# Cross attention whose weights are turned by a DMA transpose and divided after the product

## The chip, the cores and the metric

The kernel runs on one core of a Trainium2 chip. Its engines are TensorE (PE: matrix products, with their weight loads shown apart as PEld), VectorE (DVE), ScalarE (ACT), GpSimd (POOL) and SyncE (SP), which here issues transfers. The metric is the device time of one execution in microseconds, as the median of several runs.

## The reference

Sixteen sequences of 128 tokens with 128 features go through two decoder layers. Layer 0 has self attention (16 heads of 8), cross attention (8 heads of 64) and a quantised feed forward step; layer 1 has self attention, cross attention (16 heads of 64) and a mixture of 8 experts. What matters here is the cross attention of each layer:

```
q = split_heads(x @ Wq);  k = split_heads(context @ Wk);  v = split_heads(context @ Wv)
sim = einsum('bhid,bhjd->bhij', q, k) * scale
attn = softmax(sim, axis=-1)
out = einsum('bhij,bhjd->bhid', attn, v)
return out (heads side by side) @ Wo + bo
```

The second layer's is the same without scale and bias. All inputs and the output are float32.

## The kernel before

A sequence is one tile of 128 tokens by 128 features. Every sequence passes the stages self0, cross0, ffn, self1, cross1 and moe, and several sequences are under way at once. A step of the kernel is named stage.step.group: `cross1.pv.0` is the product of weights and values for the first group of eight heads in cross1. cross0 has one such group, cross1 two, so there are 48 groups in all (16 sequences by 3); the text calls one of them a unit.

The order of the steps on each engine is written out by hand in the table `ORDER` (two characters a step). At build time the class `Plan` replays the table with the costs of `all_steps()` to give each result its bank of PSUM (eight banks); the engines then run their lists in order, and semaphores make them wait.

The steps of a unit before the change are these. `s1` (PE, line 1257): scores of eight heads, 128 queries by 128 keys each. `mx` (DVE, line 980): the negative maximum of a row. `ex` (ACT, line 805): eight exponentials of 128x128. `rc` (DVE, lines 987 and 989): sum and reciprocal. `nz` (POOL, line 728): the exponentials times the reciprocal. `t` (PE, line 1270): each head's weights are turned, eight 128x128 turns into PSUM. `wT` (ACT, line 813): a copy of the turned weights to SBUF. `pv` (PE, line 1297): values times turned weights, in float32, two heads in the two halves of the array's columns ("64 columns"). `oTe` (ACT): a copy to SBUF. `y` and `z` (PE, line 1335): the output projection.

PE can divide its array into parts. The scores of the cross attention use 64 rows, those of the self attention 32, the old product 64 columns, all else the whole array; `array_parts()` says which step uses which, and `switch()` what the plan charges for a change.

The values come from `v` (PE, lines 1316 to 1318: three products of 512 columns) and `ve` (ACT copy). `AHEAD` says for how many sequences keys and values are held. SP issues the loads at the start, and then waits for each finished sequence to store it (line 669).

Of the kernel before, what the change touches and what calls it, by code (L numbers as in the profile page):

```python
# [6 lines left out]
F32 = mybir.dt.float32  # L7
# [7 lines left out]
P = 128  # L15
NSEQ = 16
SH, SD = 16, 8
XD = 64
# [13 lines left out]
AHEAD = dict(cross0=8, cross1=6)  # L32
EARLY = 4
WARM = 9

class Step:

    def __init__(self, engine, cost, after, again, bank, until, parts, once, half, first, last):
# [42 lines left out]
def all_steps():  # L82
    steps = {}

    def add(name, engine, cost, after=(), again=(), bank=None, until=None, parts=1, once=False, half=0, first=None,
            last=None):
        steps[name] = Step(engine, cost, after, again, bank, until, parts, once, half, first, last)
# [44 lines left out]
    def keys_values(L, chunks, k_w, v_w):  # L132
# [4 lines left out]
        for c in range(chunks):  # L137
            fill(f"{L}.v.{c}", 695, [*context, f"{v_w}.lo"], f"{L}.ve.{c}", [ago(f"{L}.pv.{c}", AHEAD[L])])
            add(f"{L}.ve.{c}", "ACT", 484, [f"{L}.v.{c}"])

    def cross_attention(L, source, chunks, following, biased, k_w, v_w, loads):
# [5 lines left out]
        for c in range(chunks):  # L147
            add(f"{L}.s1.{c}", "PE", 893, [f"{L}.qe.{c}", second(f"{L}.ke.{c}")], [f"{L}.t.{c}"], "S", f"{L}.ex.{c}")
            add(f"{L}.mx.{c}", "DVE", 1130, [f"{L}.s1.{c}"])
# [16 lines left out]
    add("consts", "POOL", 2700, once=True)  # L166
    for name, load, engine, hi, lo in (("ctx0", "c0", "DVE", 530, 610), ("b_k", "b_k", "DVE", 530, 610),
# [7 lines left out]
    add("self0.bi", "POOL", 412, ["self0.res", "in.more"], [ago("cross0.res", 2)])  # L175
# [21 lines left out]
    add("moe.o", "DVE", 198, ["moe.b", "moe.sm"])  # L197
    return steps
# [12 lines left out]
        "aHaJa4a4aOa4aLa6a4aHa6aQaJa6aUa6bYbqbWbWbYbWaXaObYaLb2b2aZaUbYb0aHaQaJb0b0b0a1a6aXaObaa4aLaHbcaJaZaQ"  # L211
        "bea1aUa6b2a4b0a4aXaObabWaLbjbcaUaHblaZaQaJbebnbWa1aXbYbWaOaZbwa4a1aLa4bab2bcbybjaHaUbeblbCaQbGbEbabn"
        "bYaJaXbcbJaZaLb2bja1bebwblaHa6bya4a6bQaObCa6bEbna6baaUbSbjbcbUbGaQbJblb6bebwb8bybnccb0aXbCcabQaLaJbE"
        "claZaHbGbSbUa1chbjbJcjblb6bacqb8bwcabycccla4bncsbQaOb2bWaJbcbSaQa6bCcubUbEaUchbWbwcvbybeb6cqcaaXbJcs"
        "aZb8aLbGaHcza1clcccja4cCcDcubjcvbQb2aObCaJa4bSblcHbaaUa6czbcbUbEbncCaQchbeb6bGcDbJaXcacLb8cqaLbwcHcl"
        "cjcsccbQcuaZaHbycva1bWbYbSbjbUaOblbaaJbYbCbcaUbEcLczbnaQbWcCcqcDbGchb6bebJcscjbwcaaXb8cHbyclccaZa4a1"
        "bQcua6bjaLaHcvaObCaJblbEb0aQbGbnbaczbSaUcqcCbUbcchbJcsbeaXcLbwb6cDcaaZb8a1bycHclcjccbQbWb2cucLcvbSbj"
        "bUaLaOblbCb0babEbnaQczaHbcbGaUcCcDaJb6cqb8bebJcsaXchcaaLbwcccjaZbyclaHa1cua6cvbja4bQaOblbScHa4aJbnba"
        "aQczbcaUbCcCcqbUbEcDcLchbebJcscjaXb6bGbWb8aZcacHaLa1ccclbwcubyaHcvbjbYbQaOblbSbCb2bUbEbaaQbccLbnchb6"
        "aUczb8bGcCcabebJcjbYcDcqccclcsaXcucHbwcvaZbybQaJbjaLb0b0a1blaObCa6aHbEbna6bSaQcLbYczaJbUbGbaaUcCchcD"  # L220
        "bccqb6bwbebJaXcab8cjcsccaZaLbyclcHcua1aHcvbjbYb0aOblbQb2bnbaaUbcczaQchcCaJcqbSbeaXbUcLcDcscjaOaZb6b0"
        "bCcab8bGa1aLaQbEccaUbwclbjbybYcuaXcvblbJaZb2babncHczbccqa1cCbecsbCcLcDbYbabQbcbGcHchbSbEcLbUbjcjbJbe"
# [1306 lines left out]
```

## Time and profile before

| | |
|---|---|
| median of 3 runs | 499.45 us (499.38 to 499.49) |
| span of the profiled execution | 497.5 us |
| PE busy | 488.7 us (98%) |
| ACT busy | 437.1 us (88%) |
| DVE busy | 400.1 us (80%) |
| POOL busy | 371.4 us (75%) |
| granted TensorE clock | 1.000 |

The span runs from the first to the last instruction of one profiled execution; the time of a run includes what lies around it. The profile's share of an engine is its busy time by the span. PE counts as busy from the start of a product to its modelled end, and products overlap, so how long a group of them takes is read from the start of the group to the start of what follows it. The chain of waits goes back from the last instruction, at each step to what released it.

### The profile page before, as it was taken

To read this page: it belongs to the slowest core of one execution; us is meant where nothing else is said; L and a number is where in the kernel's file an instruction comes from. 1 tells how busy PE (TensorE), PEld (TensorE's weight loads), DVE (VectorE), ACT (ScalarE), POOL (GpSimd) and SP (SyncE) were. 2 spreads that over 40 slices of the span, in tenths; PEclk is the share of its full clock that TensorE was granted. 3 is DMA by queue.
4 is the path that set the end of the run, shared out by engine and by line. 5 is a ranking of instruction groups with operands and counts; after the bars stand their busy time and mean duration, and the time that the engine had idled before them with its cause. 6 is when DMAs were issued, how large, how long until landed. Compare 5 with 4: busy or idle time off the path is not lost.

```text
span 497.5 us, 15713 instructions
## 1 busy us (share of the span) xinstructions
PE 488.7 (98%) x5510; PEld 416.8 (84%) x5510; DVE 400.1 (80%) x906; ACT 437.1 (88%) x1180; POOL 371.4 (75%) x455
## 2 busy tenths in 40 slices
PE   8999999999999999999999999999999999999996
PEld 4778887888888888889889888888888898988885
DVE  5767778897888888989898898878898687876665
ACT  5988889999998898998898898989789899989782
POOL 2876677897868887788768886976869688568754
PEclk9999999999999999999999999999999999999999
DMA  6800000000000000000000000000000000000000
GB/s 196 336 2 1 3 1 3 1 2 3 1 3 1 7 2 9 1 3 7 7 3 1 8 3 5 4 7 1 4 7 1 8 7 3 7 3 2 7 7 16
DMA packets 6460, 8.64 MB, mean 17 GB/s; under 512 B 1392, under 2 KB 4848, under 8 KB 6384
## 3 DMA queue, kind: packets, MB, share of 16 engines
q1 hardware_dynamic: 5952, 6.86, 4.1%
q8 instruction: 45, 0.74, 0.6%
q10 hardware_dynamic: 432, 0.79, 0.5%
q14 instruction: 31, 0.25, 0.2%
HBM read 6.50 MB, written 1.05 MB: 15 GB/s over the span
## 4 chain that ended last, share of the span: by engine, by line
PE 90%; ACT 4%; DVE 2%; SPq 1%; issue 1%; DMA 1%; POOL 1%; DVEq 0%; POOLq 0%; ACTq 0%
PE psum L1270 14%; PE psum L1257 10%; PE psum L1297 10%; PE psum L1213 8%; PE psum L1335 8%; PE psum L1244 6%; PE psum L1283 3%; PE psum L1461 3%; PE psum L1347 3%; PE psum L1308 2%; PE psum L1285 2%; PE psum L1316 2%; PE psum L1310 2%; PE psum L1318 2%; PE psum L1317 2%; PE psum L1309 2%
## 5 line engine op out<-in xcount | busy, mean ns | idle before, releaser
L723 POOL TENSOR_TENSOR w_self<-w_self 128x1024 f16<-128x1024 f32 x64 | 121.2, 1901 | 27.3 <-ACT w_self L794 13.8
L805 ACT ACTIVATE w_cross<-psum,row_max_cross 128x128 f32<-128x128 f32 x384 | 104.4, 408 | 5.5 <-DVE row_max_cross L980 4.6
L728 POOL TENSOR_TENSOR w_cross<-w_cross,e_rec_cross 128x1024 f32<-128x1024 f32 x48 | 91.0, 1898 | 20.6 <-DVE e_rec_cross L989 20.6
L980 DVE TENSOR_REDUCE row_max_cross<-psum 128x8 f32<-128x1024 f32 x48 | 58.0, 1215 | 13.6 <-PE psum L1257 12.8
L987 DVE TENSOR_REDUCE e_sum_cross<-w_cross 128x8 f32<-128x1024 f32 x48 | 58.2, 1213 | 4.5 <-ACT w_cross L805 4.2
L1257 PE MATMUL psum<-kT_cross,qT_cross 64*128 64x128 f32 x768 | 54.4, 283 | 0.0
L1297 PEld LDWEIGHTS psum<-w_cross,v_cross 128*64 128x64 f32 x768 | 41.1, 136 | 14.3 <-issue 11.0
L813 ACT ACTIVATE w_cross<-psum 128x1024 f32<-128x1024 f32 x48 | 49.9, 1043 | 3.3 <-PE psum L1270 3.2
L1257 PEld LDWEIGHTS psum<-kT_cross,qT_cross 64*128 64x128 f32 x768 | 46.3, 187 | 6.8 <-issue 4.9
L1297 PE MATMUL psum<-w_cross,v_cross 128*64 128x128 f32 x768 | 51.4, 278 | 0.3 <-ACT w_cross L813 0.3
L1270 PE MATMUL psum<-ident,w_cross 128*128 128x128 f32 x384 | 49.8, 274 | 0.1
L1270 PEld LDWEIGHTS psum<-ident,w_cross 128*128 128x128 f32 x384 | 43.1, 142 | 1.4 <-ACT by_head_self L770 0.3
L998 DVE TENSOR_TENSOR w_self<-psum,row_max_self 128x1024 f32<-128x1024 f32 x32 | 39.2, 1225 | 2.4
L996 DVE TENSOR_REDUCE row_max_self<-psum 128x8 f32<-128x1024 f32 x32 | 38.9, 1215 | 1.3 <-PE psum L1244 1.0
L1007 DVE SCALAR_TENSOR_TENSOR w_self<-psum,s_bound 128x1024 f32<-128x1024 f32 x32 | 37.8, 1216 | 2.5 <-PE psum L1244 2.4
L788 ACT ACTIVATE w_self<-w_self,shift 128x1024 f32<-128x1024 f32 x32 | 36.9, 1160 | 2.4 <-DVE w_self L1007 2.4
L770 ACT ACTIVATE by_head_self<-psum,head_mask 128x128 f32<-128x128 f32 x128 | 37.3, 405 | 0.0
L1244 PE MATMUL psum<-by_head_self,plain_self 32*128 32x512 f32 x256 | 36.5, 639 | 0.2 <-issue 0.2
L794 ACT ACTIVATE w_self<-psum 128x1024 f32<-128x1024 f32 x32 | 33.1, 1035 | 4.0 <-PE psum L1270 3.5
L770 ACT ACTIVATE attnT_cross<-psum 128x512 f32<-128x512 f32 x48 | 29.7, 622 | 6.8 <-PE psum L1297 6.3
L1335 PE MATMUL psum<-e_o,attnT_cross 128*128 128x128 f32 x256 | 34.3, 277 | 0.0
L1270 PE MATMUL psum<-ident,w_self 128*128 128x128 f32 x256 | 33.5, 274 | 0.5 <-DVE w_self L998 0.4
(213 smaller groups left out, 1377.0 us busy)
## 6 DMA issues: line engine op xcount, KB each, us to landing
out_dram<-x_all SPq DMA_DIRECT2D x16, 64.0 KB, 1.6
x_all<-in_x SPq DMA_DIRECT2D x1, 768.0 KB, 7.2
cT_all<-in_ctx SPq DMA_DIRECT2D x1, 768.0 KB, 9.4
e_k<-in_e_k SPq DMA_DIRECT2D x1, 512.0 KB, 4.9
e_v<-in_e_v SPq DMA_DIRECT2D x1, 512.0 KB, 5.8
e_q<-in_e_q SPq DMA_DIRECT2D x1, 512.0 KB, 8.6
e_o<-in_e_o SPq DMA_DIRECT2D x1, 512.0 KB, 9.5
m_w<-in_m_w SPq DMA_DIRECT2D x1, 512.0 KB, 8.5
```

Of the source, the lines that this page charges most:

```text
L723: pool.tensor_tensor(L.w_low[u], L.w[u][:], halves(L.w[u][:]), ALU.subtract)\
L728: pool.tensor_tensor(L.diff[u][:].rearrange("p (h k) -> p h k", h=UNIT), L.e[u][:].rearrange("p (h k) -> p h k", h=UNIT), L.e_rec[:, u, :] ...
L770: act.activation(dst, src, ACT.Copy, **scale).then_inc(emptied(i, name)[0], 1)
L805: last = act.activation(L.e[u][:, P * p:P * (p + 1)], S_[:, P * p:P * (p + 1)], ACT.Exp, bias=L.row_max[:, u, p:p + 1])
L813: act.activation(L.w[u][:], group(i, turn)[:], ACT.Copy).then_inc(taken(i, turn)[0], 1)
L980: dve.tensor_reduce(L.row_max[:, u, :], group(i, turn)[:].rearrange("p (h k) -> p h k", h=UNIT), AX_X, ALU.max, negate=True).then_inc(L.ma ...
L987: dve.tensor_reduce(L.e_sum[:, u, :], L.e[u][:].rearrange("p (h k) -> p h k", h=UNIT), AX_X, ALU.add)
L1244: last = pe.matmul(group(i, name, u)[:, 512 * half:512 * (half + 1)], L.plain[rows, :], L.by_head[rows, :, :].rearrange("p j n -> p (j n)" ...
L1257: last = pe.matmul(S_[:, at:at + P], L.qT[rows, h // 2, :], kT[rows, h // 2, i % 2, :], start=True, stop=True)
L1270: last = pe.transpose(S_[:, P * k:P * (k + 1)], L.diff[u][:, P * k:P * (k + 1)], ident[:])
L1297: last = pe.matmul(bank(i, name)[rows, P * pair:P * (pair + 1)], v[:, h, :], L.w[c][:, P * place(h):P * (place(h) + 1)], start=True, stop= ...
L1335: last = pe.matmul(bank(i, y)[:, 0:P], L.attnT[:, k, :], L.o_w[:, k, :], start=k == 0 and not with_x, stop=k == 4 * L.chunks - 1)
```

## The change

`rc`, `nz`, `t` and `wT` go. After `ex` a unit now has these steps. `hi` (ACT): the exponentials, not divided, rounded to 16 bits. `lo` (POOL): what the rounding left, also in 16 bits. `dm` (SP): one DMA transpose turns both planes, 128 by 2048 elements of 16 bits (512 KB), SBUF to SBUF, into 16 blocks of 128x128. `pv` (PE): three products a head, 24 a unit, with a turned 16-bit plane as the loaded tile and the values as the streamed columns: high plane by high values (64 columns and a column of ones, which gives the sum of the weights), high plane by low values (64), low plane by high values (65). Queries now lie on partitions. `nr` (DVE): reciprocal of the sums, and a multiplication by it. `T` (PE): four 128x128 turns of the float32 result, then `oTe` as before.

The values are held as a 16-bit high part (`ve`, ACT) and a 16-bit low part (the new `vl`, DVE), with the ones set once at the start by POOL. Values and keys are held for 6 and 4 sequences instead of 8 and 6. The result before its turn lies in the memory of the turned planes. `x_bias` shares memory with a loaded weight. The transposes and the stores are now in SP's written-out list. All tables of `ORDER` are new; one line of each stands below.

```diff
-AHEAD = dict(cross0=8, cross1=6)
+AHEAD = dict(cross0=6, cross1=4)
+TURN, TURN_TAIL = 2100, 1300
...
+            add(f"{L}.vl.{c}", "DVE", 605, [f"{L}.ve.{c}"])
...
-            add(f"{L}.ex.{c}", "ACT", 2060, [f"{L}.mx.{c}"], [f"{L}.pv.{c}"], half=1030)
-            add(f"{L}.rc.{c}", "DVE", 1401, [f"{L}.ex.{c}"])
-            add(f"{L}.nz.{c}", "POOL", 1856, [f"{L}.rc.{c}"])
-            add(f"{L}.t.{c}", "PE", 874, [f"{L}.nz.{c}"], (), "S", f"{L}.wT.{c}")
-            add(f"{L}.wT.{c}", "ACT", 914, [f"{L}.t.{c}"])
-            fill(f"{L}.pv.{c}", 873, [f"{L}.wT.{c}", f"{L}.ve.{c}"], f"{L}.oTe.{c}", [f"{L}.{'yz'[c]}"])
-            add(f"{L}.oTe.{c}", "ACT", 486, [f"{L}.pv.{c}"])
+            add(f"{L}.ex.{c}", "ACT", 2060, [f"{L}.mx.{c}"], [f"{L}.lo.{c}"], half=1030)
+            add(f"{L}.hi.{c}", "ACT", 940, [f"{L}.ex.{c}"], [f"{L}.dm.{c}"])
+            add(f"{L}.lo.{c}", "POOL", 1856, [f"{L}.hi.{c}"])
+            add(f"{L}.dm.{c}", "SP", TURN, [f"{L}.lo.{c}"], [f"{L}.T.{c}"], tail=TURN_TAIL)
+            add(f"{L}.pv.{c}", "PE", 740, [f"{L}.dm.{c}", f"{L}.vl.{c}", "ones"], (), "S", f"{L}.nr.{c}")
+            add(f"{L}.nr.{c}", "DVE", 930, [f"{L}.pv.{c}"])
+            fill(f"{L}.T.{c}", 437, [f"{L}.nr.{c}"], f"{L}.oTe.{c}")
+            add(f"{L}.oTe.{c}", "ACT", 486, [f"{L}.T.{c}"], [f"{L}.{'yz'[c]}"])
...
 ORDER = dict(
     PE=(
-        "aHaJa4a4aOa4aLa6a4aHa6aQaJa6aUa6bYbqbWbWbYbWaXaObYaLb2b2aZaUbYb0aHaQaJb0b0b0a1a6aXaObaa4aLaHbcaJaZaQ"
+        "aIaKa5aMa5aPaIa5a7a5a7aRa7bZaVbtb1aKa7bZb1aYaPbZa0b6b1aMa2aVb3b6aIaRb1aKb3b3a7bca5aYaPaMa7aIbeaKb3aR"
...
-    return ("64 columns",) * 2 if step == "pv" and L in ("cross0", "cross1") else ("", "")
+    return "", ""
...
+            def turn(L, i, u):
+                sp.wait_ge(L.e_low[u], i + 1)
+                if i:
+                    sp.wait_ge(x_full, full(i - 1, f"{L.name}.T.{u}"))
+                sp.dma_start_transpose(L.eT[u][:], L.e_parts[u][:]).then_inc(L.e_turned[u], 16)
...
-            def divide_by_sum(L, i, u):
-                pool.wait_ge(L.rec_ready[u], i + 1)
...
+            def low_weights(L, i, u):
+                pool.wait_ge(L.e_high[u], i + 1)
+                pool.tensor_tensor(L.e_parts[u][:, UN:2 * UN], L.e[u][:], L.e_parts[u][:, 0:UN], ALU.subtract)\
+                    .then_inc(L.e_low[u], 1)
...
-            def weights_by_key(L, i, u):
-                turn = f"{L.name}.t.{u}"
-                act.wait_ge(s_full, score(i, turn))
-                act.activation(L.w[u][:], group(i, turn)[:], ACT.Copy).then_inc(taken(i, turn)[0], 1)
+            def high_weights(L, i, u):
+                act.wait_ge(*taken(i, f"{L.name}.s1.{u}"))
+                if i:
+                    act.wait_ge(L.e_turned[u], 16 * i)
+                act.activation(L.e_parts[u][:, 0:UN], L.e[u][:], ACT.Copy).then_inc(L.e_high[u], 1)
...
+            def divide_by_sums(L, i, u):
+                name = f"{L.name}.pv.{u}"
+                sums = by_head(group(i, name))
+                rec = L.e_rec[:, u, :].rearrange("p (z h) -> p z h", z=2)
+                dve.wait_ge(s_full, score(i, name))
+                dve.reciprocal(rec, sums[:, :, :, XD])
+                dve.drain()
+                dve.tensor_tensor(L.attn[u].rearrange("p (z h w) -> p z h w", z=2, w=XD), sums[:, :, :, 0:XD],
+                                  rec.unsqueeze(3).broadcast_to([P, 2, UNIT // 2, XD]), ALU.mult)\
+                    .then_inc(taken(i, name)[0], 1)
...
-                pe.wait_ge(*taken(i, f"{L.name}.t.{c}"))
+                pe.wait_ge(L.e_turned[c], 16 * (i + 1))
                 room(i, name)
...
+                for h in range(UNIT):
+                    e_high, e_low = L.eT[c][:, place(h), :], L.eT[c][:, UNIT + place(h), :]
+                    at = 512 * (h // 4) + (XD + 1) * (h % 4)
+                    pe.matmul(out_[:, at:at + XD + 1], e_high, v_high[:, UNIT * c + h, :], start=True, stop=False)
+                    pe.matmul(out_[:, at:at + XD], e_high, v_low[:, UNIT * c + h, :], start=False, stop=False)
+                    last = pe.matmul(out_[:, at:at + XD + 1], e_low, v_high[:, UNIT * c + h, :], start=False, stop=True)
+                last.then_inc(s_full, 1)
```

The order on PE near the end, in the kernel before: from the projection of sequence 14 in cross1 (line 1335, `y` and `z`) to the last sequence's first product. w0 and w1 are the weights of the two head groups, v3 the values, lines 1316 to 1318 make values.

```order
L1335 MATMUL psum<-e_o,attnT_cross1 128x128 x4
L1316 MATMUL psum<-e_v_hi,cT_all_lo 128x512
L1317 MATMUL psum<-e_v_lo,cT_hi 128x512
L1318 MATMUL psum<-e_v_hi,cT_hi 128x512
L1335 MATMUL psum<-e_o,attnT_cross1 128x128 x4
L1270 MATMUL psum<-ident,w0_cross1 128x128 x8
L1448 MATMUL psum<-m_b,g_weightT 128x128
L1270 MATMUL psum<-ident,w1_cross1 128x128 x8
L1297 MATMUL psum<-w0_cross1,v3_cross1 64x128 x8
```

And in the kernel after, from the end of sequence 14's second product to the start of the last sequence's first. eT0 and eT1 hold the turned planes, and later the result that line 1367 turns; line 1404 is the projection.

```order
L1487 MATMUL psum<-m_g,moe_xnT 128x8
L1367 MATMUL psum<-ident,eT1_cross1 128x128 x4
L1519 MATMUL psum<-m_b,g_weightT 128x128
L1367 MATMUL psum<-ident,eT0_cross1 128x128 x4
L1404 MATMUL psum<-e_o,attnT_cross1 128x128 x8
L1358 MATMUL psum<-v_high3_cross1,eT0_cross1 128x65
```

The turns of the weights and the making of values have left this place; four turns of a result a group, which wait for DVE, stand ahead of the projection, and the first of 24 products of the last sequence directly behind it.

The order on ACT at the same place, before: the exponentials of the last sequence's two head groups (line 805), and the copies of its turned weights (line 813).

```order
L805 ACTIVATE w0_cross1<-psum,row_max_cross1 128x128 x8
L770 ACTIVATE attnT_cross1<-psum 128x512
L805 ACTIVATE w1_cross1<-psum,row_max_cross1 128x128 x8
L770 ACTIVATE g_weightT<-psum 128x128
L770 ACTIVATE attnT_cross1<-psum 128x512
L770 ACTIVATE v3_cross1<-psum 128x512 x2
L915 ACTIVATE psum,g_sum<-logits,g_negmax 128x8
L813 ACTIVATE w0_cross1<-psum 128x1024
```

And after; line 860 rounds the exponentials to 16 bits into e_parts.

```order
L851 ACTIVATE w0_cross1<-psum,row_max_cross1 128x128 x8
L860 ACTIVATE e_parts0_cross1<-w0_cross1 128x1024
L851 ACTIVATE w1_cross1<-psum,row_max_cross1 128x128 x8
L860 ACTIVATE e_parts1_cross1<-w1_cross1 128x1024
L816 ACTIVATE attnT_cross1<-psum 128x512 x2
```

The 1024-element step of a head group moved from behind PE's turns to directly behind its exponentials, and the two copies of sequence 14's result (attnT) stand behind both groups now.

## Rows read from the trace of the kernel before

**Rows 1.** The page: busy time of PE, and the chain that ended last, by engine.

```profile
PE 488.7 (98%) x5510; PEld 416.8 (84%) x5510; DVE 400.1 (80%) x906; ACT 437.1 (88%) x1180; POOL 371.4 (75%) x455
...
PE 90%; ACT 4%; DVE 2%; SPq 1%; issue 1%; DMA 1%; POOL 1%; DVEq 0%; POOLq 0%; ACTq 0%
```

**Rows 2.** Stretches: us, busy of PE, PEld, DVE, ACT, POOL, clock, DMA share, GB/s.

```profile
200.00:300.00 100.00, 100.00 (x1204) 87.55 (x1201) 87.50 (x195) 90.80 (x254) 82.43 (x103) 1.00 0.02 4
...
20.00:470.00 450.00, 447.75 (x5193) 385.68 (x5192) 372.27 (x808) 406.75 (x1103) 348.23 (x419) 1.00 0.02 7
470.00:497.50 27.50, 23.64 (x207) 19.21 (x205) 16.30 (x50) 16.59 (x50) 14.09 (x18) 1.00 0.04 10
```

**Rows 3.** Timeline of PE from 251 us: start, duration, engine, line, operation.

```profile
251.46 1.09 PE L1297 MATMUL psum<-w_cross,v_cross 128*64 128x128 f32 x16
252.48 0.19 PE L1283 MATMUL psum<-v_self,w_self 128*128 128x27 bf16 x1
...
253.28 0.17 PE L1285 MATMUL psum<-v_self,w_self 128*128 128x18 bf16 x1
253.31 1.07 PE L1270 MATMUL psum<-ident,w_cross 128*128 128x128 f32 x8
254.22 1.06 PE L1213 MATMUL psum<-xnT_cross,e_q 128*128 128x128 f32 x8
```

**Rows 4.** Timeline of PE from 278 us: two old products in a row.

```profile
278.64 1.97 PE L1297 MATMUL psum<-w_cross,v_cross 128*64 128x128 f32 x32
280.54 0.19 PE L1283 MATMUL psum<-v_self,w_self 128*128 128x27 bf16 x1
```

**Rows 5.** Chain of waits from 475 us: two products of 512 columns.

```profile
475.84 0.23 PE psum L1428
476.07 0.23 PE psum L1429
```

**Rows 6.** Groups by line: busy us, mean ns, idle before; steps that go.

```profile
L728 POOL TENSOR_TENSOR w_cross<-w_cross,e_rec_cross 128x1024 f32<-128x1024 f32 x48 | 91.0, 1898 | 20.6 <-DVE e_rec_cross L989 20.6
L813 ACT ACTIVATE w_cross<-psum 128x1024 f32<-128x1024 f32 x48 | 49.9, 1043 | 3.3 <-PE psum L1270 3.2
L987 DVE TENSOR_REDUCE e_sum_cross<-w_cross 128x8 f32<-128x1024 f32 x48 | 58.2, 1213 | 4.5 <-ACT w_cross L805 4.2
L989 DVE RECIPROCAL e_rec_cross<-e_sum_cross 128x8 f32<-128x8 f32 x48 | 9.7, 203 | 3.5
```

**Rows 7.** Groups by line: rows nearest to the steps that come.

```profile
L723 POOL TENSOR_TENSOR w_self<-w_self 128x1024 f16<-128x1024 f32 x64 | 121.2, 1901 | 27.3 <-ACT w_self L794 13.8
L1084 DVE TENSOR_TENSOR weighted<-psum,g_weight 128x1024 f32<-128x1024 f32 x15 | 18.3, 1222 | 1.2 <-PE psum L1429 0.4
L843 ACT ACTIVATE e_k_hi<-e_k 128x1024 fp32r<-128x1024 f32 x1 | 1.1, 1061 | 0.6 <-DMA e_k<-in_e_k 0.6
L618 DVE TENSOR_TENSOR b_k_lo<-b_k,b_k_hi 128x512 fp32r<-128x512 f32 x1 | 0.7, 693 | 0.3 <-ACT b_k_hi L843 0.3
```

**Rows 8.** The page: GB/s by slice; transfers: KB, us from issue to landing.

```profile
GB/s 196 336 2 1 3 1 3 1 2 3 1 3 1 7 2 9 1 3 7 7 3 1 8 3 5 4 7 1 4 7 1 8 7 3 7 3 2 7 7 16
...
out_dram<-x_all SPq DMA_DIRECT2D x16, 64.0 KB, 1.6
...
e_k<-in_e_k SPq DMA_DIRECT2D x1, 512.0 KB, 4.9
...
e_o<-in_e_o SPq DMA_DIRECT2D x1, 512.0 KB, 9.5
```

**Rows 9.** Groups by line: exponentials and maximum, which stay.

```profile
L805 ACT ACTIVATE w_cross<-psum,row_max_cross 128x128 f32<-128x128 f32 x384 | 104.4, 408 | 5.5 <-DVE row_max_cross L980 4.6
L980 DVE TENSOR_REDUCE row_max_cross<-psum 128x8 f32<-128x1024 f32 x48 | 58.0, 1215 | 13.6 <-PE psum L1257 12.8
```

**Rows 10.** Chain of waits near the end: the last sequence's first scores and turns.

```profile
470.69 1.09 PE psum L1257 x16
...
480.27 0.97 PE psum L1270 x8
```

More of the change, by code:

```diff
@@ L31, with __init__ @@
 BANKS = 8
-AHEAD = dict(cross0=8, cross1=6)
+AHEAD = dict(cross0=6, cross1=4)
 EARLY = 4
+TURN, TURN_TAIL = 2100, 1300
 WARM = 9
 class Step:
-    def __init__(self, engine, cost, after, again, bank, until, parts, once, half, first, last):
+    def __init__(self, engine, cost, after, again, bank, until, parts, once, half, first, last, tail):
+        self.tail = TAIL[engine] if tail is None else tail
         self.first = cost if first is None else first
@@ L85, in add @@
     def add(name, engine, cost, after=(), again=(), bank=None, until=None, parts=1, once=False, half=0, first=None,
-            last=None):
-        steps[name] = Step(engine, cost, after, again, bank, until, parts, once, half, first, last)
+            last=None, tail=None):
+        steps[name] = Step(engine, cost, after, again, bank, until, parts, once, half, first, last, tail)
     def fill(name, cost, after, until, again=(), parts=1, once=False, last=None):
@@ L166, in all_steps @@
     add("consts", "POOL", 2700, once=True)
+    add("ones", "POOL", 1000, ["consts"], once=True)
     for name, load, engine, hi, lo in (("ctx0", "c0", "DVE", 530, 610), ("b_k", "b_k", "DVE", 530, 610),
@@ L174, in all_steps @@
     self_attention("self0", "self0.st", True, "cross0", "in.first", "in.more")
-    add("self0.bi", "POOL", 412, ["self0.res", "in.more"], [ago("cross0.res", 2)])
+    add("self0.bi", "POOL", 412, ["self0.res", "in.more", since("tern.make", 1)], [ago("cross0.res", 2)])
     cross_attention("cross0", "self0.res", 1, "ffn", ["self0.bi"], "b_k", "b_v", "in.more")
@@ L346, in __init__ @@
             idle[engine] = now + cost
-            ended[i, name] = now + cost + TAIL[engine]
+            ended[i, name] = now + cost + s.tail
             self.before[i, name] = []
@@ L396, in __init__ @@
             self.diff = self.w
-            self.diff_ready = [self.sem(f"diff_ready{u}") for u in range(units)]
+            if heads == SH and width == SD:
+                self.diff_ready = [self.sem(f"diff_ready{u}") for u in range(units)]
         else:
@@ L666, in _, with store, do_step @@
                         sp.dma_start(mask[j][0:32 * j, :], mask[0][P - 32 * j:P, :]).then_inc(masks_turned, 16)
-            for i in range(NSEQ):
+            def turn(L, i, u):
[3 more added lines that the diff above has]
+                sp.dma_start_transpose(L.eT[u][:], L.e_parts[u][:]).then_inc(L.e_turned[u], 16)
+            def store(i):
                 sp.wait_ge(*emptied(i, "moe.b"))
                 sp.dma_start(out[i], x_all[:, i, :]).then_inc(stored, 16)
+            def do_step(i, name, L, step, u):
+                if step == "dm":
+                    turn(L, i, u)
+                if step == "out":
+                    store(i)
+            run("SP", do_step)
             sp.wait_ge(stored, 16 * NSEQ)
@@ L754, in do_step @@
                     cut_v(L, i)
-                if step == "lo":
+                if step == "lo" and L in (self0, self1):
                     low(L, i, u)
-                if step == "nz":
-                    divide_by_sum(L, i, u)
+                if step == "lo" and L in (cross0, cross1):
+                    low_weights(L, i, u)
                 if step == "bi":
```

199 lines of the change are left out of this document (112 added, 87 removed).

## The prediction

> **What bounds the kernel now.** I read the page's busy shares first, then the chain of waits: PE is busy 488.7 of 497.5 us, and 90% of the chain that ended last is PE, 4% ACT [rows 1]. Then the stretches: between 200 and 300 us PE has no idle time at all, while ACT is busy 90.8 and DVE 87.5 of 100 us [rows 2]. So PE's own work sets the pace, what comes off PE comes off the time, and ACT is next, about 10% behind. The end differs: from 470 us PE is busy 23.6 of 27.5 us [rows 2].
>
> The profiled span is 497.5 us and the median of the timed runs 499.45, so 1.95 us lie around the span. I keep them.
>
> **The change part by part.** A "unit" is one head group of one sequence; there are 48 (16 sequences, one group in cross0 and two in cross1). What a unit did between the exponentials and the projection is replaced.
>
> *PE, removed.* The eight turns of the weights: start of the turns to start of what follows is 253.31 to 254.22, so 0.91 us [rows 3]; 48 x 0.91 = 43.7 us. The old product: one group alone takes 251.46 to 252.48, 1.02 us [rows 3], two in a row 278.64 to 280.54, 1.90 us [rows 4]. So a product is 0.88 us, and 0.14 us goes to changing the array's division (64 columns before, whole array behind). 48 x 0.88 = 42.2 us. Together 85.9 us.
>
> *PE, added.* 24 products a unit, each with a whole 16-bit 128x128 tile to load and 65 or 64 columns to stream. The trace has no such product. Its nearest is the self attention's: 16-bit tiles of the same size with 27 and 18 columns, 32 of them from 252.48 to 253.31 [rows 3], 26 ns each. A streamed column costs 0.23 us / 512 = 0.45 ns [rows 5], so 65 columns are 29 ns. The lower bound is 26 ns, as if the columns were free; the upper is 26 + 29 = 55 ns, load and columns one after the other. The 512-column products next to each other show their loads hidden, so I take the larger of the two and 1 ns, 30 ns: 24 x 30 = 0.72 us, 48 x 0.72 = 34.6 us (30 to 63). Then four turns a unit of the result, half of the old eight: 0.455 us, 21.8 us. Added 56.4, net 29.5 us less.
>
> *PE, changes of division.* The new product uses the whole array. Counted in the two written-out orders, PE changes its division 190 times before and 156 times after; 34 x 0.14 = 4.8 us less. PE's work becomes 488.7 - 29.5 - 4.8 = 454.4 us.
>
> *ACT.* The copy of the turned weights out of PSUM goes (49.9 us), and a 16-bit copy of the exponentials comes. Nearest row: a 128x1024 copy from SBUF, 1.06 us [rows 6, 7]. 48 x 1.06 = 50.9, so ACT stays at 438 us. The copy of the values changes only its type.
>
> *DVE.* The sum (58.2) and its reciprocal (9.7) go [rows 6]. The low part of the values comes, 128x512, 0.69 us as the same subtraction takes now, or half of 1.22 us from PSUM, 0.61 [rows 7]; and a division of 128x512, likewise 0.69, behind a reciprocal of 0.20. 48 x (0.69 + 0.69 + 0.20) = 75.8 against 67.9: DVE grows from 400 to 408 us, still far from PE.
>
> *POOL.* The multiplication at 1898 ns goes [rows 6]; a subtraction of the same shape comes, 1901 ns [rows 7]. No change; setting the columns of ones is once, at the start, beside the loads.
>
> *The transposes.* 48 SBUF-to-SBUF transfers of 512 KB, issued by SP. Behind one in SP's queue stand only other transposes and the stores of finished sequences; nobody waits for a store but the end. The wait that counts is PE's, before the product. The trace has no transposing transfer. Bounds by the nearest rows: 1.6 us for a 64 KB store, 9.5 us for 512 KB among other loads; a 512 KB load that met less traffic took 4.9 us [rows 8]. With 1.6 us of fixed part and 448 KB at the 336 GB/s of the loading phase [rows 8], 1.3 us, it would be 2.9; between 2.9 and 4.9 I take 3.5 us. Queue time is no issue: 48 x 3.5 = 168 us of the span. In the middle PE has other sequences' work between the scores and the product, so the transfer hides there: what is late next is only the latency.
>
> *Latency, where it shows.* From scores to product it was maximum 1.2, exponentials 2.2 (104.4 us / 48), sum and reciprocal 1.4, multiplication 1.9, then PE's turns and ACT's copy [rows 6, 9]. Now it is 1.2 + 2.2 + 1.06 + 1.9 + 3.5 = 9.9 us. At the end PE runs out of other work. In the order after, between the last sequence's first scores and its first product stand about 5.9 us of PE work (its second scores 1.09, two products 1.4, eight turns 0.9, a projection 1.8, small steps 0.7); the two value steps that filled that place before (1.4 us) have moved ahead. So PE stands 4.0 us, and about 1 us more ahead of the last turn, whose division DVE must finish first. Before, the turns began at 480.27, 8.5 us after the first scores, with PE busy in between [rows 10]. Tail: + 5 us.
>
> *Co-bound.* Between 20 and 470 us ACT is busy 406.7 of 450 us, 90%, and PE 447.8 [rows 2]. PE's 34.3 us less would leave 415.7 us, with ACT (and its 1 us more) at 98%. An engine that takes its work in order will hardly get there: at 97% the stretch is 420 us (+5), at 95% 429 (+13). I take + 8 us. In it lies what the smaller edits can cost: keys and values held for fewer sequences, and the values' bank freed by DVE 0.69 us after ACT's copy, both at worst waits of PE for a bank or a buffer; 0 if another bank is free.
>
> **Sum.** PE 454.4, the idle time it has now 8.8, tail 5, co-bound 8: span 476.2, time 478 us. Its own range: 26 to 42 ns a product (-5 to +14), co-bound 0 to 13, tail 2 to 8: 464 to 492.
>
> **The rivals.** *Slow transposes (slower).* If a transfer takes long, PE waits in order before the product. I counted PE's work in the order after between a unit's scores and its product, with the costs of the step table, which agree with the trace where both have a step (873 ns for the old product there, 0.88 us in [rows 4]): under 10 us at 8 of 48 places, under 13 us at 17. Each us beyond 3.5 adds about 7 us, since several places share a wait; from 6.5 us on nothing is left of the gain. At the 9.5 us of [rows 8] it would be about 478 + 6 x 8 = 526 us. For it: no row shows such a transfer, and plain loads of that size took up to 9.5 us. Against it: those stood among megabytes of other loads, and from 20 us on the DMA engines are 2% busy [rows 2].
>
> The worst form is a price per 128x128 block instead of per byte: 16 blocks x 1.6 us is 26 us a transfer, 48 x 26 = 1.2 ms with SP's queue as the bound; I give it 2 of the rival's 13 in 100. The Trainium skill points there (VectorE: DVE Perf Modes, "The three transpose paths": 1309 ns for one block by DMA); by its figure it would be 21 us a transfer. The same skill (Advanced Engine Details and Errata, "X-Bar Transpose (TRN2)") calls such transfers as fast as plain ones. No run yet shows either.
>
> *ACT sets the pace.* If ACT cannot pass 93% between 20 and 470 us, the stretch is 438.5 us: 20 + 438.5 + 27.5 + 5 + 1.95 = 493. For it: [rows 2]. Against it: ACT has only 4% of the chain.
>
> *Load and product one after the other.* At 55 ns a product, 1.32 us a unit, + 29 us: 507 us, slower. Against it: [rows 5]. Half of that is in the forecast's own range.
>
> **How the numbers follow.** Forecast 75%, slow transposes 13%, ACT sets the pace 9%, load and product 3%. Faster by over 0.2% (about what a measurement of this kernel tells from no change, 1 us): 0.75 + 0.09 less 0.02 for the edge, 0.82. Within 0.2%: 0.03. Slower: 0.15. The range 463 to 500 leaves out some 13% above and 4% below.
>
> **What would show it.** Right: 24 products of a unit in 0.7 to 0.75 us; PE busy near 454 us and still nearly full between 200 and 300; transposes landing in 3 to 4 us, with short waits of PE on them, mostly in the last 25 us; ACT above 95% in the middle. Wrong: waits of PE on the transposes over 10 us in all (first rival), ACT without idle time while PE waits for its banks (second), 1.0 us or more a product group (third).

## The result, and the profile after

The changed kernel is slower: 525.14 us (median of 4 runs, 522.75 to 528.04) against 499.47 (4 runs, 499.38 to 500.27), a ratio of 1.051 with an interval of 1.047 to 1.055. I had forecast 478 us and a range of 463 to 500. The profiled run took 524.8 us, 523.0 of them span. The page of the changed kernel, where [rows 1] and [rows 8] stood:

```profile
PE 477.5 (91%) x5702; PEld 401.4 (77%) x5702; DVE 406.9 (78%) x954; ACT 439.7 (84%) x1180; POOL 382.5 (73%) x465
...
PEclk9999999997999999999999999998999999999999
...
PE 55%; issue 11%; POOL 10%; DVE 6%; ACT 5%; POOLq 5%; DMA 4%; DVEq 2%; SPq 1%; ACTq 0%
...
out_dram<-x_all SPq DMA_DIRECT2D x16, 64.0 KB, 2.4
...
eT_cross<-e_parts_cross SPq DMA_TRANSPOSE x48, 4.3
```

PE has lost 11 us of busy time and is idle for 45 us instead of 9. PE was 90% of the chain that ended last; now it is 55%, and POOL, DVE, ACT, the DMA and "issue" share the rest. That is what a chain from engine to engine looks like. The stretches of the changed kernel, for [rows 2] (us, busy of PE, PEld, DVE, ACT, POOL, clock, DMA share, GB/s):

```profile
200.00:300.00 100.00, 96.64 (x1235) 82.01 (x1234) 84.42 (x203) 91.06 (x251) 85.23 (x101) 1.00 0.37 67
20.00:495.00 475.00, 441.80 (x5433) 373.31 (x5431) 380.72 (x857) 416.37 (x1123) 363.47 (x435) 0.99 0.30 57
495.00:523.00 28.00, 18.55 (x168) 15.78 (x168) 14.12 (x51) 10.70 (x33) 11.45 (x13) 0.94 0.27 58
```

In the middle PE was full; now it misses 3 us in 100, and from 20 to 495 us 33 of 475. In the last 28 us it is idle for 9.5 us, against 3.9 of 27.5 before. What PE waits for, in the changed kernel's waits (us in total, times, longest):

```profile
PE psum L1358 <- issue: 17.1, 18, 2.1
PE psum L1358 <- DMA eT_cross<-e_parts_cross: 8.6, 5, 3.4
PE psum L1292 <- DVE v_low_cross L1037: 2.3, 1, 2.3
```

L1358 is the first of the new products. I compared each unit's landing with the start of its product: 27 of the 48 start within 0.3 us of the landing, and nearly all of the 25.7 us stands in front of these. So the 17.1 us under "issue" are the same wait for the transpose, only without a named releaser. The new groups by line, for [rows 6, 7] (busy us, mean ns, idle before; L1047 is the reciprocal):

```profile
L767 POOL TENSOR_TENSOR e_parts_cross<-w_cross,e_parts_cross 128x1024 f16<-128x1024 f32 x48 | 102.6, 2138 | 30.0 <-ACT e_parts_cross L860 29.8
...
L860 ACT ACTIVATE e_parts_cross<-w_cross 128x1024 f16<-128x1024 f32 x48 | 52.4, 1098 | 1.5 <-DMA eT_cross<-e_parts_cross 1.4
...
L1037 DVE TENSOR_TENSOR v_low_cross<-psum,v_high_cross 128x512 f16<-128x512 f32 x48 | 32.2, 680 | 6.4 <-ACT v_high_cross L934 6.1
...
L1049 DVE TENSOR_TENSOR eT_cross<-psum,e_rec_cross 128x512 f32<-128x512 f32 x48 | 33.2, 692 | 3.9 <-issue 0.4
...
L1047 DVE RECIPROCAL e_rec_cross<-psum 128x8 f32<-128x8 f32 x48 | 9.6, 199 | 22.3 <-PE psum L1360 22.1
```

The products themselves, in PE's timeline of the changed kernel (start, duration, engine, line), for [rows 3]:

```profile
262.57 0.20 PE L1358 MATMUL psum<-v_high_cross,eT_cross 128*128 128x65 bf16 x1
262.61 0.20 PE L1359 MATMUL psum<-v_low_cross,eT_cross 128*128 128x64 f16 x1
...
263.28 0.19 PE L1360 MATMUL psum<-v_high_cross,eT_cross 128*128 128x65 bf16 x1
263.39 0.17 PE L1341 MATMUL psum<-v_self,w_self 128*128 128x27 bf16 x1
```

24 of them run from 262.57 to 263.28, with 0.71 us between the first start and the last, so 31 ns a step. The products have the size I gave them. PE's waits have not.

Last, one unit's way from scores to product (cross0, sequence 8), in the timeline of the changed kernel:

```profile
235.35 1.16 PE L1319 MATMUL psum<-kT_cross,qT_cross 64*128 64x128 f32 x16
236.56 1.23 DVE L1031 TENSOR_REDUCE row_max_cross<-psum 128x8 f32<-128x1024 f32 x1 [0.51 <-PE psum L1319]
237.82 2.17 ACT L851 ACTIVATE w_cross<-psum,row_max_cross 128x128 f32<-128x128 f32 x8
239.59 1.90 POOL L762 TENSOR_TENSOR w_self<-w_self 128x1024 f16<-128x1024 f32 x1
240.18 1.05 ACT L860 ACTIVATE e_parts_cross<-w_cross 128x1024 f16<-128x1024 f32 x1
241.44 1.26 POOL L782 TENSOR_TENSOR weighted<-weighted 128x512 f32<-128x512 f32 x1
...
244.32 0.46 POOL L788 TENSOR_TENSOR weighted<-weighted,x_all 128x128 f32<-128x128 f32 x1
244.73 2.15 POOL L767 TENSOR_TENSOR e_parts_cross<-w_cross,e_parts_cross 128x1024 f16<-128x1024 f32 x1
246.91 5.56 SPq L694 DMA_TRANSPOSE eT_cross<-e_parts_cross  x2
251.31 0.19 PE L1358 MATMUL psum<-v_high_cross,eT_cross 128*128 128x65 bf16 x1
```

The scores end at 236.5 and the product starts at 251.3, 14.8 us later. The steps themselves take 11 us of that. Another 3.5 us pass between 241.2 and 244.7: the high plane is ready, but in POOL's written-out order other sequences' steps (L762, L782 to L788) stand ahead of the low plane. Over all 48 units, counted from such rows, scores to landing is 16.6 us on average (11.4 to 26.4), and 5.3 of these are waits in front of an engine: 0.3 before DVE, 0.4 and 2.5 before ACT's two steps, 1.6 before POOL, 0.5 before SP.

### The profile page after: what moved, and what is told of

It reads as the page before. It is cut to its first block, busy times and chain, and to the rows that moved or that the text cites. A ratio compares the mean times of both kernels' runs of the same rounds, so it can differ in the third digit from the quotient of the medians.

```text
span 523.0 us, 16305 instructions
## 1 busy us (share of the span) xinstructions
PE 477.5 (91%) x5702; PEld 401.4 (77%) x5702; DVE 406.9 (78%) x954; ACT 439.7 (84%) x1180; POOL 382.5 (73%) x465
## 4 chain that ended last, share of the span: by engine, by line
PE 55%; issue 11%; POOL 10%; DVE 6%; ACT 5%; POOLq 5%; DMA 4%; DVEq 2%; SPq 1%; ACTq 0%
PE psum L1319 6%; PE psum L1404 6%; PE psum L1277 5%; PE psum L1328 5%; POOL w_self L762 4%; PE psum L1308 4%; POOL e_parts_cross L767 4%; DMA eT_cross<-e_parts_cross 4%; PE psum L1367 3%; PE psum L1358 2%; POOLq L734 2%; PE psum L1532 2%; PE psum L1341 2%; PE psum L1416 2%; PE psum L1360 2%
## 5 line engine op out<-in xcount | busy, mean ns | idle before, releaser
L762 POOL TENSOR_TENSOR w_self<-w_self 128x1024 f16<-128x1024 f32 x64 | 120.8, 1897 | 20.4 <-ACT w_self L840 11.6
L767 POOL TENSOR_TENSOR e_parts_cross<-w_cross,e_parts_cross 128x1024 f16<-128x1024 f32 x48 | 102.6, 2138 | 30.0 <-ACT e_parts_cross L860 29.8
L1358 PE MATMUL psum<-v_high_cross,eT_cross 128*128 128x65 bf16 x384 | 41.7, 198 | 25.7 <-issue 17.1
L1358 PEld LDWEIGHTS psum<-v_high_cross,eT_cross 128*128 128x128 f16 x384 | 36.2, 99 | 33.6 <-issue 32.7
L860 ACT ACTIVATE e_parts_cross<-w_cross 128x1024 f16<-128x1024 f32 x48 | 52.4, 1098 | 1.5 <-DMA eT_cross<-e_parts_cross 1.4
L1360 PE MATMUL psum<-v_high_cross,eT_cross 128*128 128x65 bf16 x384 | 41.7, 196 | 0.0
L1359 PE MATMUL psum<-v_low_cross,eT_cross 128*128 128x64 f16 x384 | 41.7, 194 | 0.0
L1037 DVE TENSOR_TENSOR v_low_cross<-psum,v_high_cross 128x512 f16<-128x512 f32 x48 | 32.2, 680 | 6.4 <-ACT v_high_cross L934 6.1
L1404 PE MATMUL psum<-e_o,attnT_cross 128*128 128x128 f32 x256 | 35.4, 284 | 1.7 <-ACT attnT_cross L816 1.7
L1359 PEld LDWEIGHTS psum<-v_low_cross,eT_cross 128*128 128x128 f16 x384 | 36.3, 101 | 0.2
L1360 PEld LDWEIGHTS psum<-v_high_cross,eT_cross 128*128 128x128 f16 x384 | 36.4, 98 | 0.0
```

Source lines behind the costliest of these rows:

```text
L762: pool.tensor_tensor(L.w_low[u], L.w[u][:], halves(L.w[u][:]), ALU.subtract)\
L767: pool.tensor_tensor(L.e_parts[u][:, UN:2 * UN], L.e[u][:], L.e_parts[u][:, 0:UN], ALU.subtract)\
L860: act.activation(L.e_parts[u][:, 0:UN], L.e[u][:], ACT.Copy).then_inc(L.e_high[u], 1)
L1358: pe.matmul(out_[:, at:at + XD + 1], e_high, v_high[:, UNIT * c + h, :], start=True, stop=False)
L1359: pe.matmul(out_[:, at:at + XD], e_high, v_low[:, UNIT * c + h, :], start=False, stop=False)
L1360: last = pe.matmul(out_[:, at:at + XD + 1], e_low, v_high[:, UNIT * c + h, :], start=False, stop=True)
```

## The experiments

The theories: **T1**, the order leaves too little room for the chain to the product, so latency turns into stalls of PE; **T2**, the transposes' traffic slows the engines; **T3**, the drops of the clock are the loss; **T4**, ACT sets the pace. "Before" was run beside each and had medians of 499.3 to 499.5.

**Without the turning** (e1):

```diff
...
-                sp.dma_start_transpose(L.eT[u][:], L.e_parts[u][:]).then_inc(L.e_turned[u], 16)
+                return
...
-                act.activation(L.e_parts[u][:, 0:UN], L.e[u][:], ACT.Copy).then_inc(L.e_high[u], 1)
+                act.activation(L.e_parts[u][:, 0:UN], L.e[u][:], ACT.Identity, bias=eps[:]).then_inc(L.e_high[u], 1)
...
-                pe.wait_ge(L.e_turned[c], 16 * (i + 1))
+                pe.wait_ge(L.e_low[c], i + 1)
...
-                    e_high, e_low = L.eT[c][:, place(h), :], L.eT[c][:, UNIT + place(h), :]
+                    e_high = e_low = L.e_parts[c][:, P * place(h):P * (place(h) + 1)]
```

> Left out: the turning of the weights; the weighted sums read both parts from the unturned high plane as soon as the low plane is made. Everything else, the order of every engine included, is that of the changed kernel. T1 (the order leaves no slack for the chain high plane, low plane, transfer, product, so that latency becomes stalls of TensorE): with 4.3 to 5.4 us taken out of each of 48 chains the PE's stalls fall back, busy time stays at 477 minus the parts at the low clock, and the time falls by 30 to 45 us, to 480 to 495. T2 (the traffic of the transposes slows the engines' own instructions): the same fall, so this run tells T1 and T2 together from the rest. T3 (the clock's four drops, some 17 us at half speed, are the loss by themselves): not under 515. T4 (ScalarE sets the pace, 440 us busy with the copies of the high plane still there): not under 515.

Measured 504.37 us (502.41 to 507.29). So 21 us hang on the turning. I expected 30 to 45; 26 us above my forecast stay without it. The edit also puts a small constant into ACT's copy, which takes 1216 ns in this run instead of 1098, 5.7 us of ACT in all.

**The same, with the transposes beside it, unread** (e2; they write one tile of their own, each after the one before has landed, and the quotients get theirs):

```diff
...
+                sp.dma_start_transpose(beside[:], L.e_parts[u][:]).then_inc(L.e_turned[u], 16)
```

> Left out: as in the run without turning, the products read the unturned high plane and wait for nothing but the low plane; but the 48 transposes are issued all the same, into one tile that nobody reads. T1 (latency): within 8 us of the run without turning (480 to 500), the traffic being harmless; what may be added is the high plane's wait until a transpose has read its tile. T2 (traffic): back to 515 to 525, with longer single instructions on POOL, DVE and ACT.

506.13 us (503.23 to 506.54), 1.8 above the run without, which lies within the spread of both. So the traffic is not where the 21 us go; T2 falls.

**Half the transfer** (e3):

```diff
...
-                sp.dma_start_transpose(L.eT[u][:], L.e_parts[u][:]).then_inc(L.e_turned[u], 16)
+                sp.dma_start_transpose(L.eT[u][:, 0:UNIT, :], L.e_parts[u][:, 0:UN]).then_inc(L.e_turned[u], 16)
...
-                    e_high, e_low = L.eT[c][:, place(h), :], L.eT[c][:, UNIT + place(h), :]
+                    e_high = e_low = L.eT[c][:, place(h), :]
```

> Left out: the low plane is made and not turned; only the high plane (128 x 1024) is transposed, after the low plane is done, and stands for both parts. Issue to landing should fall from 4.3 us to between 2.2 (half of it) and 3.3 us. T1 with some 15 to 20 us of the whole for each us of latency: 490 to 510. T2 with half the packets: about half of what the run without turning gives back. T4 (ScalarE): 525, no change.

503.17 us (499.67 to 504.74). The page of this run:

```profile
L1358 PE MATMUL psum<-v_high_cross,eT_cross 128*128 128x65 bf16 x384 | 40.6, 196 | 7.2 <-DMA eT_cross<-e_parts_cross 4.9
...
eT_cross<-e_parts_cross SPq DMA_TRANSPOSE x48, 3.1
```

A transfer of 3.1 us costs no more than none at all; one of 4.3 us costs 21 us. The knee lies between the two. PE's idle time in front of the new products falls from 25.7 us to 7.2, most of what the time falls by.

**About 2 us more** (e4):

```diff
...
+                sp.dma_start(late[u][:], ident[:, 0:4]).then_inc(later[u], 16)
+                count[u] += 16
+                sp.wait_ge(later[u], count[u])
                 sp.dma_start_transpose(L.eT[u][:], L.e_parts[u][:]).then_inc(L.e_turned[u], 16)
```

> Each transpose of the changed kernel waits on SP for a 16-byte-per-partition copy in SBUF issued just before it: about 2 us more of latency per chain (bounds 1.5 to 2.6), nothing else. T1: at 15 to 20 us for each us, 550 to 565. My prediction's 7 us for each us would give 539. T2 and T4: 525 to 530, since neither the traffic nor any engine's work grows.

586.38 us (585.05 to 590.13), above every expectation. Its page, then PE's first wait:

```profile
PEclk9899897888899998999999998999798978898888
...
late<-ident SPq DMA_DIRECT2D x48, 2.0 KB, 1.7
eT_cross<-e_parts_cross SPq DMA_TRANSPOSE x48, 4.3
```

```profile
PE psum L1364 <- issue: 51.3, 23, 4.5
```

From the end of the low plane to the landing the median is 6.46 us instead of 4.36: 61 us for 2.1 us. Part of it is the clock, granted at 1.2 instead of 2.4 GHz for 86 us of the span (17 in the changed kernel, none before). Half of the 69 us more, 34, is the most that can be. So each of the 2.1 us cost 29 us as measured, and without the clock still 13.

**The transpose in two halves, the first beside POOL's step** (e5):

```diff
...
-                sp.wait_ge(L.e_low[u], i + 1)
+                sp.wait_ge(L.e_high[u], i + 1)
...
-                sp.dma_start_transpose(L.eT[u][:], L.e_parts[u][:]).then_inc(L.e_turned[u], 16)
+                sp.dma_start_transpose(L.eT[u][:, 0:UNIT, :], L.e_parts[u][:, 0:UN]).then_inc(L.e_turned[u], 16)
+                sp.wait_ge(L.e_low[u], i + 1)
+                sp.dma_start_transpose(L.eT[u][:, UNIT:2 * UNIT, :], L.e_parts[u][:, UN:2 * UN])\
+                    .then_inc(L.e_turned[u], 16)
...
```

> Nothing is left out. Each transpose is issued in two halves: the high plane's as soon as ScalarE has made it, beside POOL's 2.14 us for the low plane, and the low plane's alone behind that. T1 (only the latency beyond some 3 us costs): the low plane's transfer takes the 3.1 us of the half turn, and the time comes within 5 us of that run's 503. If the two halves queue behind each other (issue to landing of the second over 4 us), 515 to 525.

504.08 us (503.32 to 505.0), the full result at the half turn's price: the second half lands 3.2 us after issue. With all the traffic of the changed kernel and less latency, 21 us come back.

**What holds the rest? Seven eighths of the high plane's copy left out** (e6), **of the low plane's subtraction** (e7), both on top of the run without turning (in e6 POOL subtracts the one block that is left again and again):

```diff
...
-                act.activation(L.e_parts[u][:, 0:UN], L.e[u][:], ACT.Identity, bias=eps[:]).then_inc(L.e_high[u], 1)
+                act.activation(L.e_parts[u][:, 0:P], L.e[u][:, 0:P], ACT.Identity, bias=eps[:]).then_inc(L.e_high[u], 1)
...
```

```diff
...
-                pool.tensor_tensor(L.e_parts[u][:, UN:2 * UN], L.e[u][:], L.e_parts[u][:, 0:UN], ALU.subtract)\
+                pool.tensor_tensor(L.e_parts[u][:, UN:UN + P], L.e[u][:, 0:P], L.e_parts[u][:, 0:P], ALU.subtract)\
...
```

> Left out: the turning, as in the run without it, and seven eighths of the high plane: ScalarE copies 128 columns instead of 1024, POOL subtracts these again and again, the products read them for all heads. That takes some 0.8 us from each of 48 copies, 38 us of ScalarE's 440. T4 (with the turning gone, ScalarE, at 91 to 97% busy in the middle, holds TensorE up): 504 falls by 12 to 25 us, to 480 to 492. T1 (what is left is latency of the chain): 0.8 us of it at the measured slope below 3 us, which was nothing: 500 to 504.

> Left out: the turning, as in the run without it, and seven eighths of the low plane, which POOL makes for 128 columns only and nobody reads. That takes some 1.7 us from each of 48 steps of POOL, 80 us of its 383, and 1.7 us of latency from each chain, twice what the short high plane takes. T4: 500 to 504, as without the turning. T1 (latency still counts there) or POOL as the bound: 480 to 492.

495.43 (494.97 to 498.18) and 502.32 us (501.58 to 505.57). The pages of the run without turning, of e6 and of e7:

```profile
PE 472.3 (94%) x5702; PEld 398.4 (79%) x5702; DVE 403.4 (80%) x954; ACT 441.6 (88%) x1180; POOL 382.9 (76%) x465
PE 467.8 (95%) x5702; PEld 395.3 (80%) x5702; DVE 402.1 (82%) x954; ACT 411.0 (83%) x1180; POOL 381.9 (77%) x465
PE 472.0 (94%) x5702; PEld 398.1 (80%) x5702; DVE 402.9 (81%) x954; ACT 440.9 (88%) x1180; POOL 302.0 (60%) x465
```

ACT is busy 31 us less (I had expected 38; up to 5.7 of the 31 are the constant's) and 9 us are gained, less than T4 asked. POOL is busy 81 us less and 2 us are gained, within the spread of the runs. The short low plane also takes 1.7 us out of every chain (428 ns for 2139), so once the turning is gone latency of that size has no price that can be measured.

**Both left out** (e14) and **one product a head instead of three** (e13, on the run without turning):

```diff
...
-                    pe.matmul(out_[:, at:at + XD], e_high, v_low[:, UNIT * c + h, :], start=False, stop=False)
-                    last = pe.matmul(out_[:, at:at + XD + 1], e_low, v_high[:, UNIT * c + h, :], start=False, stop=True)
...
```

> Left out: the turning, as in the run without it, and two of the three products of every head; 8 instead of 24 a unit. That takes 16 x 30 ns x 48 = 23 us of work from TensorE and nothing from the others. If TensorE's own work still sets the pace once the turning is gone (it shows 98% busy in the middle): 504 falls by 18 to 24 us, to 480 to 486. If what holds it is the hand-over between four engines of nearly the same load: by 4 to 12 us, to 492 to 500.

> Left out: the turning, and seven eighths of both planes, ScalarE's copy and POOL's subtraction; 38 us less of ScalarE and 80 us less of POOL. If the two only add (9 us and 2 us as measured apart): 491 to 495. If POOL takes over as soon as ScalarE is relieved: 480 to 488.

500.81 us (496.99 to 501.76) for the few products and 495.49 (494.25 to 498.4) for both short, each just above what I had expected. With the copy short, the subtraction is worth nothing on top (495.43 without it). 23 us of PE's work are worth 3.6 us of time: PE, which set the pace before, does not set it any more, though the stretch from 200 to 300 us of the run without turning shows it nearly full:

```profile
200.00:300.00 100.00, 97.87 (x1271) 83.56 (x1268) 86.54 (x201) 94.26 (x259) 84.63 (x102) 1.00 0.02 4
```

and of the run with few products, its page first:

```profile
PE 458.2 (93%) x4934; PEld 377.3 (76%) x4934; DVE 401.2 (81%) x954; ACT 439.2 (89%) x1180; POOL 382.2 (77%) x465
...
200.00:300.00 100.00, 95.75 (x1102) 79.78 (x1099) 87.15 (x201) 94.48 (x261) 84.78 (x104) 1.00 0.01 4
```

PE's busy share falls by 2 points where about 5 points of work went. Over the whole run its busy time falls by 14 us for 23 us of work, and its idle time rises from 28.9 us to 37.0. The rest is, by all appearance, waiting that the records carry inside matmuls, whose ends are modelled.

**The order searched anew for the measured durations**, same program else: for the two halves (e8), for the changed kernel as it is (e9), and as a control for the kernel before, for its own durations (e10). The table's numbers of e9:

```diff
-TURN, TURN_TAIL = 2100, 1300
+TURN, TURN_TAIL = 1950, 2500
...
-            add(f"{L}.lo.{c}", "POOL", 1856, [f"{L}.hi.{c}"])
+            add(f"{L}.lo.{c}", "POOL", 2095, [f"{L}.hi.{c}"])
...
```

> Nothing is left out. The split transposes of the run before, with the orders of all engines searched anew for the durations that the chip showed (low plane 2.1 us, the last half turned 3.25 us behind it). T1 (the loss is the order, written for a transfer of 3.4 us and a low plane of 1.86): the stalls that the hand-overs still cost fall, and the time goes from 504 to 485 to 496, under the kernel before. If four engines at 85 to 98% leave no order without these stalls: 500 to 506, as before the search.

> The changed kernel itself, its transposes whole; only the written-out orders are searched anew for the durations that the chip showed (low plane 2.1 us, SP 1.95 us for an issue, landing 4.45 us behind the low plane). T1: the time falls from 525 by 15 to 30 us, to 495 to 510, since each product can stand further behind its scores. If the latency costs whatever the order is (buffers, banks and the single tile per unit hold the chain together): 518 to 526.

> The kernel before with its orders searched anew in the same way and for as long, for its own durations. T1 (the changed kernel's order misses the chip's durations, that of the kernel before does not): 497 to 500, no difference that can be measured. If a longer search alone brings a gain: 485 to 494.

e9: 503.23 us (502.10 to 506.76), so 22 us come back with the transfer unchanged at 4.3 us. Products within 0.3 us of their landing fall from 27 to 16 and the waits inside the chain from 5.3 to 4.1 us. e10: 502.43 us (501.22 to 502.97), 0.6% slower than before: for that kernel searching alone gains nothing, and the search missed by 3 us an order as good as the one it has, so those of e8 and e9 need not be the best either. The changed kernel searched anew for its old durations was not run; how much of the 22 us the new durations bring and how much the search is open. e8: 499.87 us (498.25 to 500.91), ratio 1.0005 (0.9992 to 1.0017): level with before, the best that kept the whole result, and short of the 485 to 496 expected.

**PE kept busy in front of the last four products** (e11, on e8), and **another order found in the same way, also with that** (e12):

```diff
...
+                if L is cross1 and i >= NSEQ - 2:
+                    keep_busy(group(i, name)[:, 0:512], 4)
...
```

> Nothing is left out. The split transposes with the searched order, and four matmuls without use (128x512, 0.23 us each) in front of each of the last four weighted sums of the second cross attention, so that TensorE does not stand idle while it waits for a transpose near the end, where its granted clock fell to 0.55 in one 5 us window. T3 (the drop of the clock follows the idle stretch and costs some 2 us there): 496 to 498.5. If the clock is not what is lost at the end: 499.5 to 501, or the dummies' own 3.7 us on top.

> As the run before it, with another order that an independent search found for the same durations. T1 with its size from the split run with the searched order: 495 to 501. A spread of more than 4 us between the two says that the orders' fine detail counts as much as the latency that they leave.

499.96 us (498.43 to 503.11) and 501.15 (499.24 to 503.41). In e11's profiled run the granted clock is 1.00 through the whole span, where e8's has half speed for 10 us, and the time is the same within its spread. The likely reading is that the drops fell where PE waits anyway; but the sixteen matmuls have a price of their own, which may hide a gain of a few us. For the changed kernel the bound is firmer: it has half speed for 17 us of its span, the run without turning for 10, so the clock explains at most 3.5 of the 21 us, and T3 falls as their cause. In e4 it may cost up to 34 us. Neither run beat the kernel before.

## Why the prediction was wrong

The **step that failed is the latency**, twice over: that the transfer hides in the middle, and the price of what does not hide. First the hiding. I summed the durations of the steps from scores to product, 9.9 us. Measured, the durations alone are 11.3 (transfer 4.6 on average and 4.3 in the median for my 3.5; low plane 2.14 for 1.9), and each step also waits in the list of its engine, 5.3 us that I had left out: 16.6 us. By my own count of PE's work between scores and product ("under 13 us at 17" of 48 places) that puts a wait at many places in the middle, where the forecast said the transfer hides.

The waits alone are nothing new, though. In the kernel before, counted in the same way from its trace, scores to turned weights in SBUF take 15.8 us, 8.8 of steps and 7.0 of waits, and only 6 of the 48 products start within 0.3 us of these weights, against 27 now. The chain has grown by under 1 us. But PE's written-out order, at the step table's costs, has 15.4 us of work on average between a unit's scores and its product, where it had 17.4. What I did not compare is the chain as it runs with the room that the new order leaves for it.

Second the price: "about 7 us" for each us, free up to 3.5 and paid back only at 6.5. By it this transfer would have cost some 6 us; it cost 21. From e3 to the changed kernel, low plane's end to landing grows from 3.12 to 4.36 us (medians) and the time by 22 us, 18 for each us, with the knee between the two. The order was laid out for 2.1 + 1.3 = 3.4 us by the change's own table (TURN and TURN_TAIL in the diff). Beyond that a late product holds everything behind it on PE, whose results the other engines wait for; that reading fits e4 and e9, and no run takes it apart further. So the first rival, slow transposes, was what happened, at 4.3 us instead of beyond 6.5; I gave it 13%. (Its sum for 9.5 us takes 8 us for each us; with the 7 it is 520, not 526.)

**Co-bound, 8 us**, was mis-sized too. Without any turning 504.4 us remain, against 478; if all of that is put down to co-bound, it is about 34 us, not 8. Of the 25 us by which that run's span exceeds my 476.2, PE's busy time has 18 (472.3 for the 454.4 that I summed) and its idle time 7; e13 says that such busy time is in part waiting. Left out one at a time, ACT's copy is worth 9 us, POOL's subtraction 2 and two thirds of PE's new products 4; a new order for the split transposes is worth another 4 (e5 to e8). These do not add up: copy and subtraction together are worth 9 again. The rest I could not assign to one engine; four engines at 76 to 94% in orders fixed beforehand is the likely reading, but it is argued, not shown. That values and keys are held for fewer sequences, which I had put into this term, no run tested.

**What held.** PE's products: 31 ns a step for my 30, and 0.73 us a unit (median, to the start of what follows) in the forecast's 0.70 to 0.75; the four turns took 0.47 us for 0.455. By the Trainium skill's 81 ns at 128 columns (TensorE: Matmul & The Clock Gate, "Back-to-back issue gap"), taken as a bound for 64 and 65 columns, a unit would have been up to 1.9 us, an estimate; the trace stays far below it. ACT: 439.7 us busy for 438. DVE: 406.9 for 408. DVE's new steps: 680 ns for the low values, 692 for the multiplication and 199 for the reciprocal, for 690, 690 and 200. The tail: 5.6 us more idle time of PE at the end for 5. The transposes' traffic, which I cost at nothing: 1.8 us, within the spread. The Trainium skill's two statements on transposes stood apart: 1309 ns for each 128x128 block (VectorE: DVE Perf Modes, "The three transpose paths") would make 21 us of 16 blocks, an estimate, and the trace shows 4.3; that they are as fast as regular transfers (Advanced Engine Details and Errata, "X-Bar Transpose (TRN2)") fits, with 4.5 to 9.7 us for plain loads of 512 KB in the same run, among other loads. The saving of 34 us in PE's work may well be there, since the steps that came took what I gave them (48 x 1.20 = 57.6 us for 56.4); it cannot be read off the time, since PE no longer sets it, and the 4.8 us in it for fewer changes of the array's division no run shows by itself.

## What to carry to other kernels

When a change puts a transfer into a chain that runs through in-order engines, sum the chain with the waits in front of each engine, which the timeline of one unit shows (here a third of the whole), not with the durations alone, and hold it against the work that the new order leaves in between. Latency was free below the room that the order left. Above it each us cost 18 us, and from 4.4 us on 29 (13 if the most that the clock can have cost is taken off). So measure the transfer first, lay the order out for the measured number, and let part of the transfer run beside the step before it. Work taken from the engine that sets the pace is worth its time only until the next chain does: the 34 us summed for PE brought nothing, even with a new order.

## What the runs showed of the hardware

- A transposing transfer of 512 KB from SBUF to SBUF (16-bit, 16 blocks of 128x128) lands 4.3 us after issue in the median (4.26 to 6.05 over 48), one of half the size 3.1. SP is busy 1.9 us (1.3 to 3.3) issuing the whole one and 1.23 us the half.
- POOL's subtraction of 128x1024, 32-bit less 16-bit to a 16-bit result, took 2138 ns for the new low plane, whose second input is a float16 tile, and 1897 in self attention, where it is the upper (bfloat16) halves of the same 32-bit tile. Why they differ no run shows.
- The granted clock fell from 2.4 to 1.2 GHz after stretches in which PE waited: for none of the span before, 17 us of it in the changed kernel, 86 in the one with 2 us more. With sixteen matmuls without use it stayed up through the profiled span; the time was 499.96 us for 499.87 without them.
